# First normalised tiles stored from the ScalarE queue, and attention's first two units rearranged

## The reference

```
x = X
x = x + 0.5 * ffn(layernorm(x))     # 64 experts, each token goes to 6 of them, and a shared one
x = x + attn(layernorm(x))          # attn(z) = (softmax(rope(Q) rope(K)^T / sqrt(32)) V) W_out + z, 16 heads of 32
x = x + 0.5 * ffn(layernorm(x))

ffn(z):  scores = sigmoid(z gate_w); the best 4 of 8 groups; the best 6 experts in them, weighted by their scores
         each expert takes up to 96 tokens: (silu(z w_gate) * (z w_up)) w_down, F = 192
         plus a shared expert of the same shape for every token
attn:    its own layernorm with weight and bias, then Q, K, V = z W_in
```

## Time and profile before

| | us |
|---|---|
| median of 3 runs (lowest, highest) | 1334.72 (1332.97, 1335.03) |
| profiled execution, its own time | 1328.23 |
| its span, first to last instruction | 1326.3 |
| PE busy | 1182.2 (89%) |
| DVE busy | 614.6 (46%) |
| ACT busy | 508.0 (38%) |
| POOL busy | 531.5 (40%) |
| mean granted TensorE clock | 0.96 |

### The profile page before, as it was taken

How to read it: one execution, slowest core, us unless ns; L and a number is a source line. 1 busy time by engine, 2 the same in 40 slices (tenths; PEclk the granted TensorE clock), 3 DMA queues, 4 the chain that set the end, 5 groups by cost and what they waited for, 6 DMA issues and landing times.

```text
span 1326.3 us, 26369 instructions
## 1 busy us (share of the span) xinstructions
PE 1182.2 (89%) x10288; PEld 773.8 (58%) x10288; DVE 614.6 (46%) x1189; ACT 508.0 (38%) x1300; POOL 531.5 (40%) x418
## 2 busy tenths in 40 slices
PE   7787999999985879999999999999997999999770
PEld 5432877776764656665556565565534777777550
DVE  7394122221224766777866976651692222222120
ACT  2222111121102358888788787772222111121100
POOL 0022455555633374534443443200023565555543
PEclk9998999999997989999999999999898999999995
DMA  9957999999997622433343424230878999999987
GB/s 334 398 174 248 317 322 324 322 318 321 318 289 205 196 74 72 95 83 80 96 101 76 113 68 109 80 124 17 296 259 286 332 323 320 320 319 317 313 216 133
DMA packets 180971, 288.71 MB, mean 218 GB/s; under 512 B 21488, under 2 KB 103792, under 8 KB 180848
## 3 DMA queue, kind: packets, MB, share of 16 engines
q1 hardware_dynamic: 147232, 218.92, 51.4%
q0 software_dynamic: 23808, 57.69, 19.1%
q10 hardware_dynamic: 9808, 10.42, 2.4%
HBM read 210.15 MB, written 55.57 MB: 200 GB/s over the span
## 4 chain that ended last, share of the span: by engine, by line
PE 49%; DVE 9%; ACT 3%; issue 3%; DMA 2%; POOL 1%; DVEq 0%; SPq 0%; ACTq 0%; POOLq 0%
PE ps L380 11%; PE ps L396 7%; PE ps L445 5%; PE ps L488 4%; PE ps L476 4%; PE ps L456 4%; PE ps L502 3%; PE ps L431 2%; PE ps L539 2%; PE ps L363 2%; DVE Mx L1142 2%; ACT ps L756 1%; PE ps L282 1%; DVE keyT L1017 1%; ACT xF L740 1%
## 5 line engine op out<-in xcount | busy, mean ns | idle before, releaser
L380 PE MATMUL ps<-bufT,gu 128*64 128x96 f32 x6144 | 292.7, 256 | 11.5 <-issue 9.2
L380 PEld LDWEIGHTS ps<-bufT,gu 128*64 128x64 f32 x6144 | 282.4, 174 | 20.6 <-issue 11.9
L1142 DVE TENSOR_REDUCE Mx<-ps 128x1 f32<-128x512 f32 x256 | 170.7, 684 | 77.2 <-PE ps L456 76.0
L756 ACT ACTIVATE ps<-ps,Mx 128x512 f32<-128x512 f32 x256 | 174.8, 685 | 49.1 <-DVE Mx L1142 43.0
L396 PE MATMUL ps<-wd,h 64*96 64x512 f32 x768 | 180.4, 602 | 5.0 <-DVE osb L1059 3.2
L711 ACT COPY bufT<-ps 128x384 f32<-128x384 f32 x128 | 60.6, 477 | 316.6 <-PE ps L363 316.6
L769 ACT ACTIVATE PT<-ps 128x512 f32<-128x512 f32 x256 | 158.4, 619 | 50.0 <-PE ps L476 47.9
L1278 POOL DMA_INDIRECT buf<-xn_d,tok x128 | 130.0, 1016 | 102.5 <-issue 58.3
L1049 DVE TENSOR_TENSOR h<-sg,ps 128x288 f32<-128x288 f32 x64 | 29.1, 454 | 303.9 <-PE ps L380 303.9
L1059 DVE TENSOR_SCALAR osb<-ps,gt 96x512 f32<-96x512 f32 x128 | 89.9, 742 | 145.7 <-PE ps L396 145.7
L456 PE MATMUL ps<-St 96*128 96x512 f32 x256 | 119.1, 483 | 8.8 <-ACT ps L756 6.3
(11 more groups left out here) (158 smaller groups left out, 1607.6 us busy)
## 6 DMA issues: line engine op xcount, KB each, us to landing
gu<-in_L_ffn_w_gate SPq DMA_DIRECT2D x128, 384.0 KB, 10.3
gu<-in_L_ffn_w_up SPq DMA_DIRECT2D x128, 384.0 KB, 11.5
wd<-in_L_ffn_w_down SPq DMA_DIRECT2D x192, 256.0 KB, 11.4
St<-HL SPq DMA_DIRECT2D x186, 128.0 KB, 2.3
qkr<-in_L_attn_W_in SPq DMA_DIRECT2D x30, 256.0 KB, 3.4
xn_d<-XN SPq DMA_DIRECT2D x24, 256.0 KB, 4.6
X<-in_L_attn_X SPq DMA_DIRECT2D x4, 1024.0 KB, 11.4
ya_d<-X SPq DMA_DIRECT2D x4, 1024.0 KB, 10.8
```

Of the source, the lines that this page charges most:

```text
L380: t = e.matmul(bk[64 * k:64 * k + 64, CAP * j:CAP * j + CAP], gu[:, 2 * k + m, c, j:F:3], f.bufT[(2 * q + k) % 4][:, c, :], start=(c == 0) ...
L756: e.activation(bk, bk, ACT.Exp, bias=Mx[:, qt, hl:hl + 1], accum_out=Dn[:, qt, hl:hl + 1]).then_inc(a_den, 1)
L1142: e.tensor_reduce(Mx[:, qt, hl:hl + 1], bank((4, 5, 7)[n % 3]), AX, ALU.max, negate=True).then_inc(a_max, 1)
```

## The change

There are two parts.

**The first tiles.** ACT issues the 16 stores of the first layer's tiles to `xn_d`, each behind its copy of that tile's transpose. SP issues the weight loads of pairs 0 and 1 right behind the loads of X, then the four `keep` transfers, then the loads of pairs 2 and 3; before pair 4 it waits until all tiles are normalised. `dve_route` waits for the last four stores four steps later, ahead of the first write to their bytes.

**Attention's head.** The loop begins at u = 0, and a straight piece stands in front of it. PE projects unit 0 and unit 1 one behind the other (unit 1 into PSUM banks 3 and 6), V's first tile, and then the 16 scores of unit 0, with V's second tile behind them. The first four scores (head 0) are computed from HL itself, three matmuls over 32 rows each, and need no stacked copy. V's third and fourth tile come in u = 0, where `pe_fill` stood. The attention tiles 4 and 5 move from u = -1 to u = 0, 6 and 7 to u = 1. On POOL the adds of tiles 4 to 7 wait for unit 0's low parts; then come unit 1's `rotate` and `rest`, `pool_weights(2)`, and only then the adds of tiles 8 to 15. Units 0 and 1 get weight buffers of their own (`wq`), both loaded behind the last expert weights and split ahead of DVE's last two evictions; `v0` is loaded behind the first filling of the ring (1 MB) and its low part is made behind the last scatter.

```
-            v = u + 2 if u > 0 and u % 4 == 2 else ...
+            v = 2 if u == 0 else u + 2 if u % 4 == 2 else ...
...
         def pe_scores(e, u, j):
-            if qt == 0:
+            if n < NDIR:
+                e.wait_ge(a_lo, 2)
+            elif qt == 0:
                 e.wait_ge(s_st[u % 3][hl], 48 * (u // 3 + 1))
...
+            if n < NDIR:
+                p = slice(32 * hl, 32 * hl + 32)
+                for m, (x, y) in enumerate(((1, 2), (1, 3), (0, 2))):
+                    t = e.matmul(bank((4, 5, 7)[n % 3]), HL[p, x, 128 * qt:128 * qt + 128], HL[p, y, :], ...
...
         def pe_attention(e):
+            for u in range(2):
+                for k in range(2):
+                    for third in range(3):
+                        pe_project(e, u, k, third)
+            for third in range(3):
+                pe_value(e, 0, third)
+            for j in range(16):
+                pe_scores(e, 0, j)
+                if j % 2:
+                    pe_busy(e, 1)
+            for third in range(3):
+                pe_value(e, 1, third)
+            pe_rows(e, 0)
-            for u in range(-2, NU + 1):
+            for u in range(NU + 1):
...
         def act_attention(e):
+            for k in range(2):
+                act_split(e, 0, k)
+            stack(e, 0, (1, 3))
+            for j in range(16):
+                act_scores(e, 0, j)
+                if j in (10, 13):
+                    act_split(e, 1, (10, 13).index(j))
+            act_log(e, 0)
+            fill(e, 0)
...
             for i in range(12, 16):
                 act_tile(e, f1, i)
+                store_xn(e, f1, i)
...
         def dve_route(e, f):
             if not f.n:
                 e.wait_ge(s_c, 32)
-                for i in range(NT - 4, NT):
-                    stored(e, f, i)
...
             e.wait_ge(f_step, 15 * f.n + 4)
+            if not f.n:
+                for i in range(NT - 4, NT):
+                    stored(e, f, i)
...
         def dve_experts(e, f):
+                if q == E // 2 and not f.n:
+                    dve_first_weights(e)
...
         def dve_attention(e):
+            for k in range(2):
+                dve_project(e, 0, k)
+                rotate(e, 0, k)
+            for k in range(2):
+                rest(e, 0, k)
+            dve_value(e, 0)
+            for j in range(16):
+                dve_scores(e, 0, j)
+                if j in (5, 7):
+                    dve_project(e, 1, (5, 7).index(j))
+                if j == 11:
+                    dve_weights(e, 2)
+            dve_lse(e, 0)
+            for i in range(4, 7):
+                dve_stat(e, i)
...
         def sp(e):
+            load(e, f1, 0)
+            load(e, f1, 1)
             for g in range(4):
-                for i in range(4 * g, 4 * g + 4):
-                    store_xn(e, f1, i)
-                if g < 3:
-                    load(e, f1, g)
                 e.wait_ge(s_x[g], 16)
                 keep(e, f1, g)
+            load(e, f1, 2)
             load(e, f1, 3)
+            e.wait_ge(f_xn, NT)
```

More of the change, by code:

```diff
@@ L679, in act_first_weights @@
         def act_first_weights(e):
+            for u in range(2):
+                e.wait_ge(s_wqk, 64)
+                e.copy(wq[u][:, 0, :, :, :], wqr[u][:, :, :, :]).then_inc(w_hi, 1)
             e.wait_ge(f_d, E)
-            e.wait_ge(s_wqk, 32)
-            e.copy(wqk[:, 0, :, :, :], qk0[:, :, :, :]).then_inc(w_hi, 1)
             e.wait_ge(s_wv, 16)
@@ L1337, in pool_attention @@
             e.wait_ge(a_add, 8)
+            for k in range(2):
+                rotate(e, 1, k)
+            for k in range(2):
+                rest(e, 1, k)
+            pool_weights(e, 2)
+            e.wait_ge(w_lo, 4)
             e.memset(St[1][96:98, 1, :, :].bitcast(F32), 1.0).then_inc(a_ones, 1)
             e.wait_ge(a_ones, 2)
-            for u in range(-2, NU + 1):
+            for i in range(8, NT):
+                pool_add(e, i)
+            e.wait_ge(a_add, NT)
+            e.memset(St[2][96:98, 1, :, :].bitcast(F32), 1.0).then_inc(a_ones, 1)
+            e.wait_ge(a_ones, 3)
+            for u in range(NU + 1):
                 far = 0 <= u + 2 < NU
@@ L1349, in pool_attention @@
                         pool_weights(e, u + 3)
-                    if u == -1 and j == 10:
-                        for i in range(8, NT):
-                            pool_add(e, i)
-                        e.wait_ge(a_add, NT)
-                        e.memset(St[2][96:98, 1, :, :].bitcast(F32), 1.0).then_inc(a_ones, 1)
-                        e.wait_ge(a_ones, 3)
                     if u == 1 and j == 15:
@@ L1424, in sp_experts @@
             load(e, f, NR - 1)
+            if not f.n:
+                value_weights(e)
             for q in range(NR, E // 2 + 1):
@@ L1456, in sp_attention @@
             again(e, 2)
-            for u in range(-2, NU + 1):
+            stack(e, 0, (2, 0))
+            fetch(e, 2)
+            again(e, 3)
+            e.dma_start(wout[:, :, :], W_out.rearrange("(c p) n -> p c n", c=4)).then_inc(s_wo, 16)
+            stack(e, 1)
+            for u in range(NU + 1):
                 for j in range(16):
@@ L1467, in sp_attention @@
                     if j == 8 and 0 <= u + 2 < NU:
-                        stack(e, u + 2, range(4) if u > -2 else (0, 2))
-                    if u == -2 and j == 9:
-                        again(e, 3)
-                        e.dma_start(wout[:, :, :], W_out.rearrange("(c p) n -> p c n", c=4)).then_inc(s_wo, 16)
+                        stack(e, u + 2)
                     if j == 0 and 0 < u < NU:
```

98 lines of the change are left out of this document (50 added, 48 removed).

## The result

| | before | after |
|---|---|---|
| median (lowest, highest), us | 1333.85 (1332.90, 1335.03), 4 runs | 1311.99 (1311.19, 1315.72), 4 runs |
| profiled execution | 1328.23 | 1311.19 |
| span | 1326.3 | 1309.4 |
| mean granted clock | 0.960 | 0.964 |

Ratio 0.9841, 95% interval 0.982 to 0.9863. The forecast of 1313.2 holds, with its range. Timed again, beside the experiments e1 and d3, the same kernel gave 1316.93 (1315.78 to 1317.97, 5 runs) and 0.9876 (0.9857 to 0.9894), 17.2 us less than the kernel before on that chip. The two intervals overlap by little; the middle of the ratios, 0.9858, is 18.9 us, and I measure the experiments against that. The interval of each ratio is 2 to 4 us wide on either side, so a difference by ratio of less than about 3 us says nothing. Ratios leave out one run of a2 (1512.12, at a granted clock of 0.736) and one of the kernel before (4016.37).

What follows compares the result with a forecast made beforehand. PE bounds attention's steady state, the DMA the experts; elsewhere PE waits at routing, scatter tail and attention's head. Terms -11.0 + 3.0 - 3.5 - 10.0 = -21.5 take 1334.7 to 1313.2 us, range 1309 to 1318.

Steps and rivals of the forecast that it cites:

- Routing, -11.0 forecast: Start of routing: DVE's 14.4 us wait for a store goes, ACT's issues cost 3.4, so -11.0.
- The cost of ACT's issues: Tiles ahead of the routing: ACT's store issues delay the logits by 3.4 us, ends 0 and 13.
- the step of 6 us: Routing: a store landing within 6 us of its issue leaves DVE no wait at its first write to the bytes.
- Experts +3.0: Experts' stage: `v0` adds 1 MB ahead of 24 pairs of weights, between 0 and 3.2 us, taken as +3.0.
- tail -3.5: Scatters behind the experts: 2.1 for a slow issue and 1.5 for half a megabyte, -3.5, ends 0 and -7.
- The slow scatter (-2.1): Experts' tail: the issue of 3.49 instead of 1.42 beside DVE's wv subtraction goes, 2.1 us gained.
- PE's last matmul moves by 8 only: End of the experts, a sign to check: PE's last matmul moves by 8 us only, not by 11.
- Head -10.0: Attention's head, up to the rows of unit 1: 10.0 us shorter, ends -13.6 and -5.
- This stall goes: Attention's head: PE's 5.90 us stand at unit 2's projection, behind POOL's adds and `pool_weights`, disappears.
- ACT waits 3.6 for unit 2's rotation: Attention's head: POOL's adds delay unit 2's `rotate` to 484.2, so ACT waits 3.6 us, PE behind it.
- the head gives half: Rival, attention's head: low clock or a further wait leaves the term at -5, 1318.2; chance 0.14.
- all covers hold: Rival: ACT's issues take 0.33 and vanish, unit 2's rotation is not late, -28.5, 1306.2; chance 0.22.

Runs made afterwards that it cites:

- e1: Changed kernel with tiles 4 to 7's normalisation in unit 0's score loop, POOL's memsets and the projection weights' subtractions moved later; median 1312.05, 0.983 of the kernel before.
- d3: Changed kernel without the six fill matmuls behind unit 1's second tile; median 1312.47, 0.985 of the kernel before.
- a2: Changed kernel, ACT still storing, with DVE's wait for the last four stores back ahead of the routing's first step; median 1319.51, 0.9894 of the kernel before.
- a1: Changed kernel with its store part undone: SP stores, DVE waits at the routing's first step; median 1328.55, 0.9967 of the kernel before.
- a3: Changed kernel with the 16 stores back on SP's queue, DVE's wait left ahead of the fifth step; median 1324.72, 0.9948 of the kernel before.
- b1: Changed kernel with V's 1 MB of weights loaded at the end of the experts instead of their start; median 1314.30, 0.9861 of the kernel before.
- x1: Changed kernel with V's 1 MB of weights loaded four times during the experts, 3 MB more; median 1319.76, 0.9921 of the kernel before.
- c1: Changed kernel with DVE's projection-weight subtractions behind the last scatter and V's behind the last halving of xT; median 1313.70, 0.9869 of the kernel before.
- d1: Changed kernel with POOL's two memsets moved from ahead of unit 2's first rotation to behind it; median 1312.49, 0.9866 of the kernel before.
- d2: Changed kernel with DVE's statistics of tiles 4 to 7 reordered, 4 and 5 ahead of V's first copy; median 1313.23, 0.9864 of the kernel before.

## Why the prediction was right, and where it was not

The sum was -21.5; the medians are 21.9 apart in the first timing and 17.2 in the second, the two profiled executions 17.0. So the closeness of the total (1313.2 for 1312.0) is in part luck: the first measurement came out low, and the middle of both is 18.9. Also, before's single profile has a last stage of 307.4, when 13 profiles with the same code there have 309.2 to 314.8 (mean 311.2). The changed kernel's own has 309.3, so this stage, which the change does not touch, makes 1.9 of what the profiled executions lack against the medians; the rest is not found.

- **Routing, -11.0 forecast, -13.8 measured.** The mechanism is right: a1, a2 and a3 show queue and wait, each by itself. The cost of ACT's issues is the term that was mis-sized: 3.4 (its own figures, 12 x 0.27, make 3.2) was taken from issues where both queues were at work, but the trace shows 0.33 each, and it counted issue and copy one behind the other, where they start together (41.80 and 41.79). The end at 0 was right. The landing was put at 3 to 4 us and is 6.1, and the step of 6 us that was to cover it was used up to the last 0.1. With a wait at the first step this would have cost 4.2.
- **Experts +3.0 and tail -3.5, together -0.5; measured +1.4 in the profile, +0.6 as a mean of five.** The sum is near, both terms are wrong. Counting the megabyte as +3.0 in one stage and -1.5 in the next took two places for two costs. b1 shows no effect of the place beyond the scatter, x1 that a megabyte costs 1.9 to 2.8. Over both stages the change only adds half a megabyte, unit 1's Q and K weights, and x1 prices that at 1.0 to 1.4. The slow scatter (-2.1) didn't go, since the subtractions for `wq` came beside another scatter: the prediction asked what waits behind the moved subtraction and not what POOL would be doing beside it. With the slow issue cured (c1) no gain could be measured either, so the 2.1 is not shown to be there to gain. "PE's last matmul moves by 8 only" failed, it moved by 13.1.
- **Head -10.0; measured -5.9 in the profile, -4.1 as a mean of seven profiles with this code (121.3 us to unit 2's rows, 125.4 before); a1 by its ratio says -4.4, with experts and tail in it.** Up to the logarithm it held: 10.3 earlier, counted from attention's start, against 9.4. Then two steps failed. "This stall goes": the 5.90 went, but a wait of 2.5 for V's second bank took its place, which a PE queue with V ahead of the projection makes, and I had not looked up who frees that bank. "ACT waits 3.6 for unit 2's rotation" named the wrong engine: DVE's chain beside POOL made 3.2 of wait, as d1 and e1 show. And unit 1 with its second tile was priced at 0.7; it takes 2.6 more than before at the same granted clock of 1.00, and 4.2 more at 0.94 to 0.95.
- The rival "the head gives half" had the head's size right (-5), by its further waits and not by its low clock (V's second tile took 3.23 us), and "all covers hold" had the issues right. The forecast held since errors of opposite sign met: 2.8 us more from the routing stood against 1.1 to 1.9 less from experts and tail and 4.1 to 5.9 less from the head.

## What to carry to other kernels

When a DMA that frees a buffer sits behind megabytes in its queue, another engine's queue issues it sooner (6 us here) and takes a third or more off its landing (10.0 to 6.1 us), and moving the wait down to the first write of the bytes takes the rest; try both, here they added. When you move a small DVE step, write down what POOL runs at its new place. When a rearrangement takes a stall away, list for each PSUM bank on the path who frees it and what stands ahead of that in its queue, before you book the gain.

## What the runs showed of the hardware

- **DVE's small steps end with POOL's operation.** An 8-element `TENSOR_TENSOR` on DVE that normally takes 0.17 us ended at 471.32, POOL's `TENSOR_TENSOR` at 471.30; a `TENSOR_SCALAR` and POOL's next operation at 472.68 and 472.66; the log-sum's subtraction at 456.25 and POOL's at 456.23. A `TENSOR_SCALAR` does so beside a memset too (d1: 470.06 and 470.03), a `TENSOR_TENSOR` does not (d2: 0.17 us at 468.04, beside a memset from 468.04 to 469.84). `TENSOR_REDUCE` from PSUM keeps its 0.6 to 0.7 throughout. This agrees with the Trainium skill, page "SBUF — State Buffer", on the pair of ports that VectorE and GpSimd lock for a whole instruction.
- **A POOL scatter's issue waits at its start for a DVE subtraction of two SBUF inputs, and not after that.** In all eleven profiles with the subtractions in the tail, the slow issue ends 1.29 to 1.30 us behind the end of a subtraction (before: 406.33 and 405.04; changed: 387.32 and 386.03), and 1.29 is the usual 1.42 without its first 0.13. In a2, x1, d2 and d3 it was the first of two subtractions that held it, and the last 1.29 us ran beside the second without taking longer (d2: subtractions from 383.67 to 384.90 and from 384.81 to 386.03, issue from 384.37 to 386.19). An issue that had begun 0.12 us before a subtraction kept its 1.42 (the changed kernel again, 386.19 and 386.31). The inference of the Trainium skill, page "SBUF — State Buffer", section "Who interferes with whom", that a `tensor_tensor` leaves descriptor generation alone is not contradicted by this; the wait is at the start. What the issue does in its first 0.13 us no row shows.
- **Same code, other length.** With the same work in it, unit 1 takes 29.4 us in two profiles and 31.0 in nine, with the granted clock at 1.00 or at 0.94 to 0.95; the last stage takes 307.4 to 314.8 us. On a kernel of this size a single profile tells a stage's change of 2 us only if the stage is read by itself, and in several profiles.
